# ScalarE's tables ahead of tokens in a convolution, and the token stores issued on SyncE's queue

## The reference

```python
dtA = A * dt[:, None];  dA = (1 + dtA/2) / (1 - dtA/2)           # (256, 64) complex
K = 2 * einsum('chn,hnl->chl', C*B, exp(log(dA)[:, :, None] * arange(256))).real    # tokens (16, 256, 256)
h = K
h = h + attention_block(layernorm(h))    # linear attention, 16 heads; MLP 256 -> 1024 -> 256 with gelu
h = h + tree_ffn(layernorm(h))           # soft decision tree of depth 8, 256 leaves, output projection
```

## Time and profile before

| | us |
|---|---|
| median of 3 runs | 582.16 (580.17 to 582.64) |
| the profiled execution: its own time | 583.05 |
| its span, from first to last instruction | 581.3 |
| busy in the span: PE, DVE, ACT, POOL | 456.3, 351.6, 286.7, 184.9 |
| convolution: DVE's first multiplication to its last sum | 41.87 to 114.18 |
| DVE's first statistics of the tokens | 124.49 |

### The profile page before, as it was taken

How to read it: one execution, slowest core, us unless ns; L and a number is a source line. 1 busy time by engine, 2 the same in 40 slices (tenths; PEclk the granted TensorE clock), 3 DMA queues, 4 the chain that set the end, 5 groups by cost and what they waited for, 6 DMA issues and landing times. The chain is left out here.

```text
span 581.3 us, 11097 instructions
## 1 busy us (share of the span) xinstructions
PE 456.3 (79%) x3664; PEld 409.8 (71%) x3664; DVE 351.6 (60%) x820; ACT 286.7 (49%) x571; POOL 184.9 (32%) x159
## 2 busy tenths in 40 slices
PE   0056567517899999689999998998999989989654
PEld 0055467415777777678898897997988979989543
DVE  5857675735767765434657558467566485663732
ACT  4522533215776667354646644564466446544310
POOL 0696866411211111123250711614307106141200
PEclk9987976866999999979999999999999999999966
DMA  3804447350114112010100200202002001010101
GB/s 119 262 0 110 122 127 220 91 162 36 38 38 100 37 41 69 36 37 1 38 1 1 72 0 1 71 0 72 0 0 72 0 0 36 0 37 1 36 1 37
DMA packets 37816, 30.86 MB, mean 53 GB/s; under 512 B 19488, under 2 KB 31136, under 8 KB 37792
## 3 DMA queue, kind: packets, MB, share of 16 engines
q1 hardware_dynamic: 18688, 22.04, 12.3%
q10 hardware_dynamic: 19104, 8.52, 4.9%
HBM read 17.97 MB, written 12.58 MB: 53 GB/s over the span
## 5 line engine op out<-in xcount | busy, mean ns | idle before, releaser
L1003 DVE TENSOR_TENSOR gl<-PS,gh 128x512 fp32r<-128x512 f32 x64 | 44.2, 690 | 78.1 <-ACT gh L662 51.8
L659 ACT ACTIVATE PS<-PS,fc1bias 128x512 f32<-128x512 f32 x64 | 42.0, 657 | 94.2 <-PE PS L272 94.2
L270 PE MATMUL PS<-fc2h,gh 128*128 128x256 f32 x256 | 74.4, 291 | 5.5 <-DVE gl L1003 4.7
L272 PE MATMUL PS<-fc2l,gh 128*128 128x256 f32 x256 | 72.3, 283 | 0.0
L271 PE MATMUL PS<-fc2h,gl 128*128 128x256 f32 x256 | 72.3, 282 | 0.0
L1134 PE MATMUL PS<-M,Wa 128*64 128x64 f32 x512 | 43.4, 269 | 34.1 <-DVE M L830 28.0
L450 POOL TENSOR_SCALAR pst<-mv 128x4 f32<-128x4 f32 x16 | 3.7, 230 | 206.8 <-DVE pst L987 206.8
L1134 PEld LDWEIGHTS PS<-M,Wa 128*64 128x64 f32 x512 | 39.2, 174 | 36.2 <-DVE M L830 36.0
L270 PEld LDWEIGHTS PS<-fc2h,gh 128*128 128x128 f32 x256 | 48.6, 190 | 10.2 <-DVE gl L1003 5.5
L270 PE MATMUL PS<-x2Th,fc1h 128*128 (+1 forms) x128 | 52.4, 409 | 2.1 <-DVE x2Tl L974 2.1
L271 PE MATMUL PS<-x2Th,fc1l 128*128 (+1 forms) x128 | 50.9, 398 | 0.0
(11 more groups left out here) (191 smaller groups left out, 1332.1 us busy)
## 6 DMA issues: line engine op xcount, KB each, us to landing
h_scratch<-tokev ACTq DMA_DIRECT2D x16, 256.0 KB, 2.9
h<-h_scratch SPq DMA_DIRECT2D x16, 256.0 KB, 3.6
q_scratch<-qe ACTq DMA_DIRECT2D x16, 256.0 KB, 2.1
qf<-q_scratch SPq DMA_DIRECT2D x16, 256.0 KB, 2.9
out_tokens<-outb SPq DMA_DIRECT2D x16, 256.0 KB, 2.2
craw<-in_c_ri SPq DMA_DIRECT2D x16, 128.0 KB, 2.2
craw<-in_c_ri SPq DMA_DIRECT2D x32, 64.0 KB, 2.4
fc1raw<-in_fc1T SPq DMA_DIRECT2D x1, 1024.0 KB, 7.0
```

Of the source, the lines that this page charges most:

```text
L270: pe.matmul(dst, ah, bh, start=start, stop=False, **kw)
L272: return pe.matmul(dst, ah, bl, start=False, stop=stop, **kw)
L659: act.activation(bank(j % 2), bank(j % 2), ACT.Gelu, bias=fc1bias[:, j:j + 1]).then_inc(gact, 1)
L1003: dve.tensor_tensor(gl[:, j % 2, :], bank(j % 2), gh[:, j % 2, :].bitcast(F32), ALU.subtract).then_inc(gldone, 1)
```

## The change

ACT's `tables_out` is split: the copy of `XY` keeps the name, and the copy of `X` into `M` becomes `m_unshifted`. ACT's order for each chunk n is then `tables_out(n+2)`, `operands(n+2)`, `m_unshifted(n+2)`, `token_out(n)`; chunks 0 and 1 are opened ahead of the loop, and the last two closed behind it. DVE's wait for the matmuls of chunk n-2 moves from before the multiplications to before the sum. `store_h0` goes from ACT to SP, where `store_h0(n-2)` follows `load_c(n)`. The first half's 8 `load_h0` are no longer between the coefficient loads: 4 stand behind `store_h0(13)`, 4 behind `store_h0(14)`, and `store_h0(15)` is behind all 8.

```diff
@@ SP
+            def store_h0(n):
+
+                sp.wait_ge(tokout, CREDIT + n + 1)
+                sp.dma_start(h0s[n * CH:(n + 1) * CH].rearrange("(g f) c d a -> (f c d) g a", f=2),
+                             tokev[:, n % 2, :, :]).then_inc(h0st[n % 2], 16)
+
...
-            for n in range(2, CHUNKS - 5):
+            for n in range(2, CHUNKS):
                 load_c(n // 2, n % 2)
-            load_c((CHUNKS - 5) // 2, (CHUNKS - 5) % 2)
+                store_h0(n - 2)
             for par in range(2):
                 sp.wait_ge(h0st[par], CREDIT + 16 * (PAIRS // 2))
-            load_h0(0, 0)
-            load_c((CHUNKS - 4) // 2, (CHUNKS - 4) % 2)
-            load_h0(0, 1)
-            load_h0(0, 2)
...
-            load_c((CHUNKS - 1) // 2, (CHUNKS - 1) % 2)
-            load_h0(0, 7)
+            for g in range(GROUPS // 2):
+                load_h0(0, g)
+            store_h0(CHUNKS - 2)
+            for g in range(GROUPS // 2, GROUPS):
+                load_h0(0, g)
+            store_h0(CHUNKS - 1)
             for par in range(2):
                 sp.wait_ge(h0st[par], CREDIT + 16 * PAIRS)
@@ ACT
+            def m_unshifted(it, par):
+                n = 2 * it + par
                 act.wait_ge(tokmm, CREDIT + n - 1)
                 apart(act)
                 act.activation(M[:, par, :, :, 0], X[:, bass.ds(n * CH, CH), :], ACT.Copy).then_inc(m0done, 1)
...
-            def store_h0(it, par):
...
-            def chunks(it, more):
-
-                operands(it, 1)
-                tables_out(it, 1)
-                token_out(it, 0)
-                store_h0(it, 0)
-                if more:
-                    operands(it + 1, 0)
-                    tables_out(it + 1, 0)
-                token_out(it, 1)
-                store_h0(it, 1)
-
-            operands(0, 0)
-            tables_out(0, 0)
+            def opened(it, par):
+                tables_out(it, par)
+                operands(it, par)
+                m_unshifted(it, par)
+
+            def closed(it, par):
+                token_out(it, par)
+
+            for par in range(2):
+                opened(0, par)
             with act.Fori(0, PAIRS - 1) as it:
-                chunks(it, True)
-            chunks(PAIRS - 1, False)
+                for par in range(2):
+                    opened(it + 1, par)
+                    closed(it, par)
+            for par in range(2):
+                closed(PAIRS - 1, par)
@@ DVE, products
                 dve.wait_ge(xyld, CREDIT + n + 1)
-                dve.wait_ge(tokmm, CREDIT + n - 1)
                 dve.wait_ge(vdone, CREDIT + 3 * n)
...
+                dve.wait_ge(tokmm, CREDIT + n - 1)
                 dve.wait_ge(vdone, CREDIT + 3 * n + 2)
                 dve.tensor_tensor(M[:, par, :, :, 1:NE], Ma, Mb[:, :, :, :], ALU.add).then_inc(vdone, 1)
```

## The result

The changed kernel takes 597.61 us (median, 597.27 to 598.57) against 581.61 beside it: ratio 1.028, 95% interval 1.0253 to 1.0306. The forecast was 594.0, in a range of 586 to 602. The profiled execution took 597.63 us, 14.6 us more than that of before (583.05), with a span of 595.8.

A forecast was written before the change was run, and what follows sets the result against it. Before, a two-chunk loop through ACT's order bounds the convolution; after, a one-chunk loop of 5.43 us. Thirteen turns, then store 15 behind eight loads, delay the second half's loads by 11.8 us: 582.16 to 594.0, range 586 to 602.

The forecast's parts named there:

- The loop: Convolution: token copy, SP's store, next coefficient loads, ACT's copies, next token copy; 5.43 us a chunk against 4.52.
- SP's issues: Convolution, each turn on SP: store's issue 0.46 us, first coefficient load to second 0.39, second to third 0.51.
- The landing's 2.6: Convolution, each turn: third coefficient load's issue to landing takes 2.6 us, with a 256 KB store just ahead.
- The hold: Handover: store 15 waits in SP's queue behind eight first-half loads, landing at 133.0 instead of 129.1.
- about 6 us after its issue: Handover, sign in the changed profile: the last store's landing comes this long after its issue.
- The sum: Handover: loop and queue put the second half's loads at 133.05 instead of 121.20, +11.8 us; the rest rides along.
- Tokens(13): Convolution: ACT's token copy of chunk 13 at 119.7, thirteen turns of 5.43 us after that of chunk 0 at 49.14.
- the step to the median: Whole kernel: profiled execution lay 0.89 us above the median, so 594.9 profiled became 594.0.
- Rival 1: Convolution: loads not late, DVE sets the pace at 3.36 us a chunk, 567 us in all; chance 0.05.
- break-even at 4.52 us a turn: Convolution: a loop over this makes the kernel slower, under it faster.
- Rival 2: Handover: loop is there, but store 15 is not held by the eight loads; +7.9, 590.0 us; chance 0.18.
- Rival 3: Convolution: the store slows the loads behind it every turn; loop 6.0 to 6.1, about 602 us; chance 0.12.

The follow-up runs named there:

- order_alone: Kernel before with only the new order on ACT and DVE, stores still issued by ACT: 568.25 us, ratio 0.9749 to the kernel before.
- ahead: Changed kernel with SP issuing the coefficient loads one chunk ahead of the stores: 568.34 us, ratio 0.9762 to the kernel before.
- stores_alone: Kernel before with only the stores moved to SP, old order on ACT and DVE: 577.28 us, ratio 0.9932 to the kernel before.
- ahead_last: Changed kernel, coefficient loads one chunk ahead, only one first-half load before stores 14 and 15: 563.56 us, ratio 0.9689 to the kernel before.
- handover_after: Changed kernel with only one first-half load before stores 14 and 15, the other seven behind: 593.71 us, ratio 1.0205 to the kernel before.
- two_stores: Changed kernel with each chunk's store cut in two DMAs of 128 KB: 601.48 us, ratio 1.0327 to the kernel before.
- after_again: Changed kernel unaltered, run again: 596.81 us, ratio 1.0256 to the kernel before.
- handover_again: Changed kernel with only one first-half load before stores 14 and 15, run again: 595.53 us, ratio 1.0239 to the kernel before.
- early: Changed kernel with the first half's 8 loads two behind each of stores 10 to 13: 597.96 us, ratio 1.028 to the kernel before.
- order_last: Kernel before with new ACT and DVE order, stores on ACT, one first-half load ahead of the last store's landing: 565.94 us, ratio 0.972.

## Why the prediction was right

*The loop.* Right in place and mechanism: ACT idle before its copy of `craw`, ended by the DMA, 12 times; SP waiting for the token copy 15 times. Its size was short: 5.43 us against 5.69. The term is SP's issues. I took the spacing of loads issued alone, 0.39 and 0.51 us; directly behind a store they were 0.57 (101.56 to 102.12) and about 0.59 (half of 1.18). That is 0.26 a turn, 3.4 us in thirteen. The landing's 2.6 was about right: from the third issue at 102.7 to ACT's copy at 105.64 it is 2.9, ACT's 0.1 in it; in the shortest turns 2.6.

*The hold.* Right in mechanism, wrong in size: 3.9 us were forecast and 1.4 measured. The term is the work of chunk 15. Store 15 was to be issued 6.1 us after store 13 and came 7.6 after it (123.93 to 131.54), when most of the queue had drained. POOL's first product of chunk 15 took 2.41 us instead of 1.6, PE began 0.4 us after the second one's end (126.67 to 127.09), and its matmuls, at a granted clock of 0.50 from 127 to 131, took 3.8 to the token copy at 130.92. The statement "about 6 us after its issue" was wrong, at 4.1.

*The sum.* Tokens(13) were 3.6 us later than predicted (123.27, 119.7), chunk 15 took 1.5 more, and the hold was 2.5 shorter, so the last store landed 2.6 us later: 135.6 against 133.0. The errors partly cancel, and that is luck: the forecast, 3.6 us under the median, is better than its parts. Of these 3.6, 0.9 come from the step to the median: the profiled execution of before lay 0.89 above its median, that of the changed kernel at it. Rival 1 fell, and order_alone and ahead show what it would have been: near the pace of DVE (3.3 to 3.6 us a chunk), once the loop is gone. Its break-even at 4.52 us a turn agrees with stores_alone, which at 4.12 was faster. Rival 2, no hold, lies between: the hold was a third of the forecast. Rival 3 is half true: the transfer of the store does delay the loads in some turns. From the third issue to ACT's copy it is 2.6 us in the shortest turns and 3.1 in the longest (about 57.2 to 60.28), 0.5 more.

*PE and the clock.* The clock in the convolution fell from 0.78 to 0.71, and that shows in the last chunk only, since the new loop does not contain PE; the loop of the kernel before did. In ahead_last the stretch to the last token copy is at 0.93:

```profile
41.50:98.80 57.30, 35.71 (x1024) 33.71 (x1024) 53.53 (x50) 25.04 (x63) 49.02 (x32) 0.93 0.51 138
```

DVE is busy for 53.5 of 57.3 us there; that is the bound that the change was in a position to reach.

## What to carry to other kernels

What a store on a queue that also carries loads cost here was mostly the wait in front of it: 28.6 us for a wait that moves nothing. The wait is not dear by itself; with ACT's old order (stores_alone), or with the loads one chunk ahead, it stands in the same stream and does no harm. Before moving a DMA to another engine, write down what each engine's stream waits for in program order and follow it until it closes. Here the loop one chunk long, with a load's issue and landing in it, took 5.7 us a turn, where the chunks of ahead and order_alone followed at 3.3 and 3.6. The repair is one place in the order, loads one iteration ahead of the stores, and a transfer that ends a stage must not stand behind loads that nobody needs yet.

## What was not expected of the hardware

**DVE holds up POOL.** Chunk 15's first product on POOL, in the changed kernel and in handover_after:

```profile
122.80 2.41 POOL L414 TENSOR_TENSOR Wa<-craw,U 128x768 f32<-128x768 f32 x1 [2.71 <-PE PS L1129]
```

```profile
120.27 2.73 POOL L413 TENSOR_TENSOR Wa<-craw,U 128x768 f32<-128x768 f32 x1 [2.38 <-DMA craw<-in_c_ri]
```

In chunks 0 to 14 of the changed kernel the same product took 1.59 us on average. In both traces DVE was in a subtraction with both inputs in SBUF when chunk 15's began; in the changed kernel:

```profile
122.04 1.76 DVE L754 TENSOR_TENSOR qkvl<-qkvraw,qkvh 128x1536 fp32r<-128x1536 f32 x1
```

It ended at 123.80, 1.00 us after POOL's start, and POOL's product was 0.82 longer. In handover_after DVE's ended 1.31 us after POOL's start: 1.14 longer. In two_stores 0.66 and 0.49. In after_again it was 1.05 and 0.87, in handover_again 1.34 and 1.16. In early it had ended before, and the product took 1.57. So POOL did next to nothing until DVE was through. The Trainium skill ("SBUF — State Buffer", Who interferes with whom) says that an operation of VectorE with two SBUF inputs and one of GpSimd that reads SBUF exclude each other for a whole instruction; these traces agree. The chunks' own multiplications have one input in PSUM, and beside them POOL kept its 1.59.

It happened the other way round as well. DVE's small copy of `ones` into `vt` takes 0.16 us in the changed kernel. In ahead, ahead_last, order_alone and order_last it began beside POOL's last product, took 1.48, 0.99, 0.65 and 0.41 us, and each time ended 0.02 to 0.03 us after that product.

**An issue's cost depends on what was issued before it.** The first coefficient load held SP for 0.34 us alone and 0.53 directly behind a store; the second one followed 0.57 instead of 0.39 us later. In early, with two first-half loads between the store and it, it held SP for 0.39.
